# z and products held in PSUM until split, query mixes on VectorE, x words in a ring, new instruction orders

## The chip, the cores and the metric

The program runs on one core of a Trainium2 chip. The metric is the device time of one execution in microseconds (us). Engines are TensorE (PE, matmuls; its weight loads are PEld), VectorE (DVE), ScalarE (ACT), GpSimd (POOL) and SyncE (SP, which here only issues DMAs). Each has its own instruction stream, carried out in order; they meet at semaphores.

## The reference

The input is x of shape (16, 1024, 256) in float32. For each of the 16 batches, with layernorm (LN) over the last axis:

```
x = x + LN(attention(LN(x)))       # q, k, v from W_qkv (768 x 256) and its bias; softmax(q k^T / 16) v
x = x + LN(ffn(LN(x)))             # silu(x Wg^T) * (x Wu^T), then Wd^T; hidden 768, weights int32 / 127
```

## The kernel before, in words

**Two words for a float32.** Matmuls run on float16. Each float32 operand is split into a high word (`h`, a copy to float16) and a low word (`l`, the float32 minus the high word), and a product takes three matmuls: high*high, low*high, high*low (`passes` and `pairs`, line 1026). For nearly every tensor one engine thus writes the high words (ScalarE, the functions named `*_high`), another subtracts to get the low words (GpSimd `*_low`, some on VectorE), and SP issues a DMA transpose of each (`turn_*`).

**Attention.** Q and K are folded into one 256x256 matrix A, so scores are z times x, where z = A x + bias. `project_z` (two banks of PSUM, one per half `dj` of the 256 rows) makes z for half `g` of a batch. From batch 2 on, the scores are made by Winograd's form of Strassen's scheme: seven block products instead of eight, for each pair of 128-row tiles (`pair_first` makes four, `pair_second`, `pair_third` and `pair_last` one each; line 1177). It needs sums of blocks of x (`mix_keys`, words `t`) and of z (`mix_queries`, words `q`). ScalarE copies products from PSUM (`copy_m1`, `copy_u2`, `copy_u3`), VectorE adds others and finds the row maxima (`sum_*`, line 857), ScalarE does `exp`, then `p_high`, `p_low`, `turn_p`. `attend` multiplies the transposed probabilities by x in four units `u` of 12 matmuls per half batch: `u // 2` is the half of the 256 columns (bank 6 or 7, `OB`), `u % 2` the half of the 1024 keys. `o_high` and `o_low` split the result, `project_v` multiplies by the value matrix.

**FFN.** `y_*` functions do the layernorm between. `gate_up` makes one of six hidden chunks `c` of a half batch: gate in PSUM bank `bank`, up in `bank + 1`, eight matmuls of 512 columns. `silu` (ScalarE) writes hf in SBUF, `h_mul` (VectorE, line 963) multiplies it by up, `h_high` and `h_low` split it. `h_low` of chunks 2 and 5 (`HL_ON_VECTOR`) is VectorE's, the others GpSimd's (line 495). `down` (24 matmuls of 256 columns) multiplies by Wd into banks 4 and 5 (`TB`), then `d_stats`, `d_norm`, `d_add`, `add_bias`, `store`.

**z before the change.** `z_high` (ScalarE) writes zTh from PSUM with scale and bias; `z_float` (VectorE, line 842) writes the same in float32 to zw in SBUF; `z_low` (GpSimd, line 405) makes zTl from it; `mix_queries` (GpSimd, lines 445 to 451, four operations of 256 columns) mixes zw in place; `q_high` (ScalarE) and `q_low` (GpSimd, line 422) split it. PSUM banks 0 to 3 hold products or gate_up results, 4 and 5 hold V and down tiles, 6 and 7 hold attention outputs or gate_up results; so one who writes a bank waits for its last reader, which is the wait written in each call.

**Orders.** No planner runs in the kernel: the order of every engine is written out by hand, call by call, for the first batches, a loop `for b in range(1, 13)` and the last three batches. One turn of the loop does the gate stage and FFN of batch b, the scores of batch b + 1 and b + 2 and the attention of b and b + 1. In the loop TensorE's list says what covers what: for pair 3 it was pair_second, pair_third, project_z, pair_last, gate_up with nothing between the first three, each of which waits for a ScalarE copy of the product before.

**x.** `X` is a ring of four half batches in float32 for the residual (`reload`, `x1_add`, `d_add`, `add_bias`, `store`); `xh`, `xl` are the words of x, two whole batches each; `xs` is the normalized x.

Of the kernel before, what the change touches and what calls it, by code (L numbers as in the profile page):

```python
# [44 lines left out]
def sandwich(nc, x_d, wqkv_d, b_d, wg_d, wu_d, wd_d, out_d):  # L45
# [8 lines left out]
    with ctx:  # L54
# [6 lines left out]
        X = two("X", [128, 4, D], f32, 4)  # L61
        xs = sb("xs", [128, NT, D])
        xh, xl = two("xh", [128, NT, D]), two("xl", [128, NT, D])
# [61 lines left out]
        xs_in, x_turned, X_in = sems("xs_in", 2), sems("x_turned", 2), sems("X_in", 4)  # L125
        p_turned, y_turned, stored = sems("p_turned", 3), sem("y_turned"), sems("stored", 4)
# [11 lines left out]
        pv_done, dn_done = sems("pv_done", 4), sems("dn_done", 2)  # L138
# [58 lines left out]
        stage = ((half_words(X[0], 1536), half_words(X[1], 1536)), (half_words(X[2], 1536), half_words(X[3], 1536)),  # L197
# [55 lines left out]
        def pv_wait(e, b, g):  # L253
            e.wait_ge(pv_done[1], 2 * b + g + 1)
            e.wait_ge(pv_done[3], 2 * b + g + 1)

# [12 lines left out]
        def turn_x(s, b, g, low):  # L269
            k, gs = b % 2, slice(4 * g, 4 * g + 4)  # L270
# [6 lines left out]
            s.engine.dma_start_transpose(dst[k][:, gs, :, :].rearrange("p t d n -> p (t d) n"),  # L277
                                         src[k][:, gs, :].rearrange("p t d -> p (t d)")).then_inc(x_turned[g], 16)

        def turn_t(s, b, g, low):  # L280
# [3 lines left out]
            s.wait_ge(bv_ready, 1)  # L284
            scores_read(s, b - 1, 4)
# [3 lines left out]
        def reload(s, b, g):  # L289
            k = (2 * b + g) % 4  # L290
            s.wait_ge(stored[k], 32 * (b // 2))
            if b < 2:
                s.wait_ge(ffn_turned[b], 32)
# [20 lines left out]
        def store(s, b, g, pair):  # L314
            k, pr = (2 * b + g) % 4, slice(2 * pair, 2 * pair + 2)
# [5 lines left out]
        def store_last(s, part):  # L321
            ts = (slice(0, 3), slice(3, 4))[part]
            s.wait_ge(last_out[part], (3, 1)[part])
            s.engine.dma_start(out_d[B - 1, :, :].rearrange("(p t) d -> p t d", t=NT)[:, 4 + ts.start:4 + ts.stop, :], X[3][:, ts, :]
                               ).then_inc(stored[3], 16)
# [52 lines left out]
        def x_hat_first(tile):  # L378

            return X[2 + tile // 4][:, tile % 4, :]  # L380

# [6 lines left out]
        def x_low(p, b, g):  # L388
            k, gs = b % 2, slice(4 * g, 4 * g + 4)
# [5 lines left out]
            pv_wait(p, b - 2, 1)  # L395
            src = xs[:, gs, :] if b else X[2 + g][:, :, :]
            p.engine.tensor_tensor(out=xl[k][:, gs, :], in0=src, in1=xh[k][:, gs, :], op=ALU.subtract
# [19 lines left out]
        def q_low(p, b, g):  # L417
            n = 2 * (b - 2) + g
            p.wait_ge(qh_done, n + 1)
            p.wait_ge(mix_z, 4 * (n + 1))  # L420
# [17 lines left out]

        def mix_queries(e, b, g):

            w = zw[:, :, :].rearrange("p j (u h n) -> p j u h n", h=2, n=128)
            a11, a12, a21, a22 = w[:, 0, :, 1, :], w[:, 1, :, 1, :], w[:, 0, :, 0, :], w[:, 1, :, 0, :]
            n = 4 * (2 * (b - 2) + g)
            zl_wait(e, b, g, 1)
            e.engine.tensor_tensor(out=a22, in0=a22, in1=a21, op=ALU.add).then_inc(mix_z, 1)
            e.wait_ge(mix_z, n + 1)
            e.engine.tensor_tensor(out=a21, in0=a21, in1=a11, op=ALU.subtract).then_inc(mix_z, 1)
            e.wait_ge(mix_z, n + 2)
            e.engine.tensor_tensor(out=a11, in0=a22, in1=a11, op=ALU.subtract).then_inc(mix_z, 1)
            e.wait_ge(mix_z, n + 3)  # L450
            e.engine.tensor_tensor(out=a12, in0=a12, in1=a11, op=ALU.subtract).then_inc(mix_z, 1)
# [109 lines left out]
        def x_high(a, b, g):  # L561
# [5 lines left out]
            pv_wait(a, b - 2, 1)  # L567
            a.engine.activation(xh[b % 2][:, gs, :], xs[:, gs, :] if b else X[2 + g][:, :, :], ACT.Copy).then_inc(xh_done, 1)

        def z_high(a, b, g, bank):  # L570
            a.wait_ge(cb_ready, 1)
            scores_read(a, b - 1, 2 * (g + 1))
            for dj in range(2):
# [33 lines left out]
        def q_high(a, b, g):  # L607
            n = 2 * (b - 2) + g
            a.wait_ge(mix_z, 4 * (n + 1))
# [18 lines left out]
        def o_high(a, b, g, dh):  # L628
            n = 2 * b + g
            a.wait_ge(pv_done[2 * dh + 1], n + 1)  # L630
# [3 lines left out]
        def y_hat(a, b, g, half):  # L634
# [3 lines left out]
            for t in (2 * half, 2 * half + 1):  # L638
                a.engine.activation(yn[:, t, :], X[n % 4][:, t, :], ACT.Identity, bias=nb3[:, t:t + 1], scale=rs3[:, t:t + 1]
# [8 lines left out]
        def silu(a, b, g, c, bank):  # L648
# [3 lines left out]
            if n > 2:  # L652
# [3 lines left out]
        def h_high(a, b, g, c):  # L656
# [4 lines left out]
            a.engine.activation(hTh[g][:, c, :], hf[:, n % 3, :], ACT.Copy).then_inc(hh_done, 1)  # L661

        def add_bias(a, b, g, pair):
            n = 2 * b + g
            k = n % 4
# [6 lines left out]
        def last_bias(a):  # L672
# [5 lines left out]
            for t in range(4):  # L678
                a.engine.activation(X[3][:, t, :], X[3][:, t, :], ACT.Identity, bias=c2[:, n % 4, t:t + 1]).then_inc(last_x, 1)
# [156 lines left out]
        def z_float(v, b, g, bank):  # L836
            v.wait_ge(ql_done, 2 * (b - 2) + g)
            for dj in range(2):
# [4 lines left out]
                                       op0=ALU.mult, op1=ALU.add).then_inc(zw_done, 1)  # L843

# [114 lines left out]
        def h_mul(v, b, g, c, bank):  # L959
# [51 lines left out]
        def last_add(v, *ts):  # L1011
            v.wait_ge(last_rs, 1 + (ts[0] == 3))
            for t in ts:
# [5 lines left out]
                v.engine.scalar_tensor_tensor(out=X[3][:, t, :], in0=last_at(t), scalar=rs4[:, t:t + 1], in1=X[3][:, t, :],  # L1019
# [106 lines left out]

        def first_scores_left(t, banks):
# [86 lines left out]
        def attend(t, b, g, u, free=None, also=None):  # L1214
            dh, q0, k = u // 2, 4 * (u % 2), b % 2
# [9 lines left out]
            passes(t, OB[dh], pairs(*((xh[k][:, kt, ds], xl[k][:, kt, ds], PTh[g][:, kt, :], PTl[g][:, kt, :])  # L1225
                                      for kt in range(q0, q0 + 4))), q0 == 0, q0 == 4).then_inc(pv_done[u], 1)
# [57 lines left out]
        def _(engine):  # L1284
# [1307 lines left out]
```

## Time and profile before

| what | us |
|---|---|
| median of 3 runs (lowest, highest) | 1403.44 (1403.24, 1407.39) |
| the profiled execution, its own time | 1403.3 |
| its span | 1401.4 |
| TensorE busy | 1325.5 (95%) |
| GpSimd busy | 1124.2 (80%) |
| ScalarE busy | 1015.5 (72%) |
| VectorE busy | 956.6 (68%) |

The profiled execution is 0.14 us below the median, so it stands for it. The mean granted TensorE clock is 0.996. A busy time is that of the engine's instructions with overlaps counted once. An idle time in brackets behind an instruction, with a releaser, is time in which the engine stood still before it.

### The profile page before, as it was taken

How to read it: one execution, taken by the hardware profiler on the slowest of the kernel's cores; microseconds unless marked ns; L12 is line 12 of the kernel's file. 1: busy time of each engine (PE TensorE's matmuls, PEld its weight loads, DVE VectorE, ACT ScalarE, POOL GpSimd, SP SyncE). 2: the span in 40 equal slices, each digit the busy share in tenths (PEclk: the TensorE clock that was granted, in tenths of full speed). 3: DMA queues.
4: the chain of work that ended last, by engine and by line, in shares of the span. 5: the costliest groups of instructions: out<-in, count | busy, mean ns of one | idle time of the engine just before them, and what ended most of it. 6: DMA issues, size and time to landing. Idle time of an engine off the chain costs nothing. (4 is left out here: it accounts for less than half of the span.)

```text
span 1401.4 us, 23224 instructions
## 1 busy us (share of the span) xinstructions
PE 1325.5 (95%) x7210; PEld 697.5 (50%) x7210; DVE 956.6 (68%) x2504; ACT 1015.5 (72%) x1602; POOL 1124.2 (80%) x1225
## 2 busy tenths in 40 slices
PE   8988999999999999999999999999999999999997
PEld 4443554454554545455445544545445454555554
DVE  7975576776667666666676766767676677756666
ACT  5657687777777777777777777777777777776746
POOL 5488688797987979979798797978979799795645
PEclk9999999999999999999999999999999999999999
DMA  4876757566566655676556765666666466646612
GB/s 143 195 151 121 128 102 140 115 129 126 120 122 135 129 99 121 128 136 129 112 119 119 130 136 115 127 121 124 136 120 140 103 121 128 128 91 121 143 31 77
DMA packets 492111, 171.97 MB, mean 123 GB/s; under 512 B 473041, under 2 KB 475473, under 8 KB 491986
## 3 DMA queue, kind: packets, MB, share of 16 engines
q1 hardware_dynamic: 491184, 169.67, 60.8%
q8 instruction: 59, 0.97, 0.3%
q10 hardware_dynamic: 802, 0.79, 0.2%
q14 instruction: 66, 0.54, 0.1%
HBM read 36.70 MB, written 16.78 MB: 38 GB/s over the span
## 5 line engine op out<-in xcount | busy, mean ns | idle before, releaser
L459 POOL TENSOR_TENSOR Pl<-P,Ph 128x1024 f16<-128x1024 f32 x96 | 210.1, 2194 | 59.8 <-ACT Ph L626 30.9
L963 DVE SCALAR_TENSOR_TENSOR hf<-S,sc,hf 128x512 f32<-128x512 f32 x192 | 139.8, 745 | 131.8 <-ACT hf L654 117.6
L1026 PE MATMUL S<-PTh,xh 128*128 128x512 f16 x512 | 194.1, 379 | 2.3 <-DMA PTl<-Pl 2.3
L1026 PE MATMUL S<-PTl,xh 128*128 128x512 f16 x512 | 194.1, 379 | 0.0
L1026 PE MATMUL S<-PTh,xl 128*128 128x512 f16 x512 | 194.1, 379 | 0.0
L654 ACT ACTIVATE hf<-S,sc 128x512 f32<-128x512 f32 x192 | 126.9, 682 | 79.5 <-POOL hTl L495 61.6
L495 POOL TENSOR_TENSOR hTl<-hf,hTh 128x512 f16<-128x512 f32 x128 | 166.7, 1317 | 8.5 <-ACT hTh L661 6.1
L1026 PE MATMUL S<-Wh,hTh 128*128 128x256 f16 x768 | 170.3, 273 | 0.8 <-POOL hTl L495 0.7
L1026 PE MATMUL S<-Wh,hTl 128*128 128x256 f16 x768 | 170.3, 273 | 0.0
L1026 PE MATMUL S<-yTh,Gh 128*128 128x512 f16 x384 | 146.8, 382 | 14.5 <-DMA yTl<-yl 6.6
L619 ACT ACTIVATE P<-P,nmx,sc 128x1024 f32<-128x1024 f32 x112 | 138.0, 1233 | 27.3 <-DVE nmx L863 27.1
L360 POOL TENSOR_TENSOR rs<-rs,mhalf 128x4 f32<-128x4 f32 (+2 forms) x160 | 146.0, 912 | 13.3
L626 ACT ACTIVATE Ph<-P 128x1024 f16<-128x1024 f32 x128 | 133.0, 1050 | 32.0 <-DMA PTl<-Pl 31.0
L1026 PE MATMUL S<-yTl,Gh 128*128 128x512 f16 x384 | 146.6, 382 | 0.0
L1026 PE MATMUL S<-yTh,Uh 128*128 128x512 f16 x384 | 146.1, 381 | 0.0
L1026 PE MATMUL S<-yTl,Uh 128*128 128x512 f16 x384 | 146.0, 380 | 0.0
L857 DVE CUSTOM_DVE_ANT_0 P<-S,P 128x512 f32<-128x512 f32 x112 | 76.4, 683 | 80.3 <-ACT P L598 79.0
L661 ACT ACTIVATE hTh<-hf 128x512 f16<-128x512 f32 x192 | 114.8, 620 | 9.8 <-DVE hf L963 9.6
L926 DVE SCALAR_TENSOR_TENSOR S<-S,rinv,bvb 128x256 f32<-128x256 f32 x128 | 53.4, 485 | 99.9 <-PE S L1026 99.9
L356 POOL TENSOR_SCALAR rs<-mv,sc 128x2 f32<-128x2 f32 (+2 forms) x96 | 35.2, 366 | 95.6 <-DVE mv L939 84.4
L857 DVE CUSTOM_DVE_ANT_0 P<-S,P,mxh 128x512 f32<-128x512 f32 x112 | 84.0, 750 | 26.0 <-PE S L1177 17.6
L495 DVE TENSOR_TENSOR hTl<-hf,hTh 128x512 f16<-128x512 f32 x64 | 86.1, 1346 | 13.1 <-ACT hTh L661 13.1
(202 smaller groups left out, 3357.4 us busy)
## 6 DMA issues: line engine op xcount, KB each, us to landing
xs<-in_L_attn_t SPq DMA_DIRECT2D x32, 512.0 KB, 4.6
X<-in_L_attn_t SPq DMA_DIRECT2D x32, 512.0 KB, 4.2
out_x<-X SPq DMA_DIRECT2D x62, 256.0 KB, 3.3
PTh<-Ph SPq DMA_TRANSPOSE x128, 3.5
PTl<-Pl SPq DMA_TRANSPOSE x128, 3.3
hTh<-in_L_ffn_w_up SPq DMA_DIRECT2D x1, 768.0 KB, 8.6
hTl<-in_L_ffn_w_gate SPq DMA_DIRECT2D x1, 768.0 KB, 5.0
hTl<-in_L_ffn_w_down SPq DMA_DIRECT2D x1, 768.0 KB, 6.7
```

Source lines behind the costliest of these rows:

```text
L356: p.engine.tensor_scalar(rs, var, scalar1=eps, scalar2=mul, op0=ALU.add, **({} if mul is None else {"op1": ALU.mult})).then_inc(g_step, 1)
L360: return p.engine.tensor_tensor(out=rs, in0=rs, in1=mhalf[:, 0:rs.shape[1]], op=ALU.pow)
L459: p.engine.tensor_tensor(out=Pl[:, m % 3, :], in0=P[:, m % 4, :], in1=Ph[:, m % 3, :], op=ALU.subtract).then_inc(pl_vector if i in PL_ON_V ...
L495: p.engine.tensor_tensor(out=hTl[g][:, c, :], in0=hf[:, n % 3, :], in1=hTh[g][:, c, :], op=ALU.subtract).then_inc(hl_vector if c in HL_ON_ ...
L619: a.engine.activation(P[:, m % 4, :], ps[:, bank:bank + 2, :].rearrange("p a n -> p (a n)") if b < 2 else P[:, m % 4, :], ACT.Exp, bias=nm ...
L626: a.engine.activation(Ph[:, m % 3, :], P[:, m % 4, :], ACT.Copy).then_inc(ph_done, 1)
L654: a.engine.activation(hf[:, n % 3, :], ps[:, bank, :], ACT.Silu, scale=sc2[:, 3:4]).then_inc(silu_done, 1)
L661: a.engine.activation(hTh[g][:, c, :], hf[:, n % 3, :], ACT.Copy).then_inc(hh_done, 1)
L857: return v.engine.tensor_tensor_reduce(out=out, in0=ps[:, bank, :], in1=other, scale=1.0, scalar=least, op0=ALU.add, op1=ALU.max, accum_ou ...
L926: v.engine.scalar_tensor_tensor(out=y_tile(t), in0=y_tile(t), scalar=rinv[:, b % 2, 4 * g + t:4 * g + t + 1], in1=bvb[:, :], op0=ALU.mult, ...
L963: v.engine.scalar_tensor_tensor(out=hf[:, n % 3, :], in0=ps[:, bank + 1, :], scalar=sc2[:, 4:5], in1=hf[:, n % 3, :], op0=ALU.mult, op1=AL ...
L1026: done = t.engine.matmul(out, s, m, start=(start and i == 0), stop=(stop and i == len(terms) - 1))
```

## The change

1. **z stays in PSUM.** From batch 2 on `z_float` and `z_low` give way to `z_bias` (VectorE, in place in PSUM), `z_high` (ScalarE, now a plain copy that waits for z_bias) and `z_rest` (VectorE). 
2. **`mix_queries` moves from GpSimd to VectorE**, reads z in PSUM and writes zw: five operations of 256 columns in place of four.
3. **Chunks 2 and 5:** `h_mul` writes its product back into the up bank, `h_high` reads it there and `h_rest` (VectorE) takes the place of VectorE's `h_low`.
4. **`attend` is cut in eight `attend_part`s** of 6 matmuls, `project_z` in two `z_part`s (12 each, one bank), so that they can be put between products. The z of half 0 goes to banks 6 and 7 (free when `o_low` is done), that of half 1 to banks 2 and 3.
5. **Rings.** xh and xl become rings of five half batches (2 KB more per partition each), X a ring of three (4 KB less). Setup data that lay in X[3] lies in tTl.
6. **New orders** on all five engines. TensorE executes the same matmuls as before.

```diff
+        def z_bias(v, b, g, bank):
+            for dj in range(2):
+                v.wait_ge(z_done, 4 * b + 2 * g + dj + 1)
+                v.engine.tensor_scalar(ps[:, bank + dj, :], ps[:, bank + dj, :], scalar1=ZS, scalar2=cb[:, dj:dj + 1],
+                                       op0=ALU.mult, op1=ALU.add).then_inc(zw_done, 1)
+
+        def z_rest(v, b, g, bank):
...
+                v.engine.scalar_tensor_tensor(out=zTl[:, dj, g * 512:(g + 1) * 512], in0=ps[:, bank + dj, :], scalar=1.0,
+                                              in1=zTh[:, dj, g * 512:(g + 1) * 512], op0=ALU.mult, op1=ALU.subtract
+                                              ).then_inc(zl_done, 1)
+
+        def mix_queries(v, b, g, bank):
...
+            zl_wait(v, b, g, 1)
+            v.wait_ge(qh_done, n)
+            v.wait_ge(ql_done, n)
...
+            v.engine.tensor_copy(w[:, 0, :, 0, :], at_z(*a21)).then_inc(mix_z, 1)
+            v.wait_ge(mix_z, 5 * n + 1)
+            term(a22, at_z(*a22), w[:, 0, :, 0, :], ALU.add)
+            term(a21, w[:, 0, :, 0, :], at_z(*a11), ALU.subtract)
+            v.wait_ge(mix_z, 5 * n + 2)
+            term(a11, w[:, 1, :, 0, :], at_z(*a11), ALU.subtract)
+            v.wait_ge(mix_z, 5 * n + 4)
+            term(a12, at_z(*a12), w[:, 0, :, 1, :], ALU.subtract)
```

TensorE's loop, from pair 3 to the next batch's first pair, before and after (`free` waits in brackets):

```
before: pair_first 3, project_v 1, pair_second 3, pair_third 3, project_z 0 [u3_copied], pair_last 3,
  gate_up 0,0 | down | gate_up 0,1 0,2 | down | gate_up 0,3 [zw_done] | project_z 1 [silu, hmul 3]
  gate_up 0,4 0,5 1,0 1,1 [zw_done] 1,2 1,3 1,4 1,5 | down | down | pair_first 0
after:  pair_first 3, project_v 1, pair_second 3, z_part 0,0, pair_third 3, z_part 0,1, gate_up 0,0,
  pair_last 3 | down | down | gate_up 0,1 0,2 0,3 0,4 [mix_z 4 and 5] | z_part 1,0 [silu 4], z_part 1,1 [hmul 4]
  gate_up 0,5 [silu 3, hl_vector 1] 1,0 1,1 [hl_vector 2] 1,2 | down | gate_up 1,3 [mix_z 9 and 10]
  gate_up 1,4 1,5 [silu, hmul 10] | down | pair_first 0 [silu 11, hmul 11, silu 12, hl_vector 4],
  attend_part 4, pair_second 0, attend_part 0, pair_third 0, attend_part 6 5 1 7, pair_last 0
```

In SP's list `turn_y` of batch 0 moves from behind two reloads and two setup transposes to directly behind the transposes of x of batch 2, and `reload` of half 1 of batch 1 moves far back. In ScalarE's loop three `h_high` of half 1 and `q_high` of half 1 move ahead of the next batch's products; GpSimd's `y_low` moves ahead of `x_low`, and `q_low` of half 1 ahead of the second pair's products.

## Rows read from the trace of the kernel before

**Rows 1.** Page, busy time of each engine over the span:
```profile
PE 1325.5 (95%) x7210; PEld 697.5 (50%) x7210; DVE 956.6 (68%) x2504; ACT 1015.5 (72%) x1602; POOL 1124.2 (80%) x1225
```

**Rows 2.** Windows: stretch, length, then busy us of each engine, granted clock, DMA:
```profile
595.90:681.60 85.70, 81.65 (x445) 42.76 (x446) 58.44 (x156) 64.22 (x103) 72.40 (x78) 1.00 0.64 124
618.00:655.00 37.00, 36.20 (x214) 20.55 (x212) 26.86 (x54) 28.50 (x45) 35.07 (x37) 1.00 0.68 133
...
107.00:124.00 17.00, 12.53 (x46) 5.10 (x47) 4.01 (x8) 10.13 (x17) 11.27 (x11) 0.80 0.74 126
```

**Rows 3.** Timeline of TensorE (start, duration, instruction): unbroken runs, first and last:
```profile
565.17 0.27 PE L1026 MATMUL S<-Wh,hTh 128*128 128x256 f16 x1
...
570.19 0.27 PE L1026 MATMUL S<-Wh,hTh 128*128 128x256 f16 x1
...
577.05 0.38 PE L1026 MATMUL S<-PTh,xh 128*128 128x512 f16 x1
...
582.01 0.38 PE L1026 MATMUL S<-PTh,xl 128*128 128x512 f16 x1
```

**Rows 4.** Timeline of TensorE: its stops in one turn of the loop:
```profile
595.86 0.38 PE L1177 MATMUL S<-tTh,qTh 128*128 128x512 f16 x1 [1.16 <-issue]
...
615.61 0.39 PE L1177 MATMUL S<-tTh,qTh 128*128 128x512 f16 x1 [0.69 <-ACT P L592]
...
617.21 0.38 PE L1026 MATMUL S<-xTh,Ah 128*128 128x512 f16 x1 [0.78 <-ACT P L598]
...
621.41 0.39 PE L1026 MATMUL S<-yTh,Gh 128*128 128x512 f16 x1 [0.80 <-DMA yTl<-yl]
...
670.89 0.39 PE L1177 MATMUL S<-tTh,qTh 128*128 128x512 f16 x1 [0.50 <-ACT P L586]
...
681.59 0.38 PE L1177 MATMUL S<-tTh,qTh 128*128 128x512 f16 x1 [1.16 <-issue]
```

**Rows 5.** Timeline of GpSimd: the q_low ahead of the first stop of rows 4:
```profile
593.63 2.13 POOL L422 TENSOR_TENSOR qTl<-zw,qTh 128x1024 f16<-128x1024 f32 x1
```

**Rows 6.** Groups of VectorE (busy us, mean ns of one):
```profile
L963 DVE SCALAR_TENSOR_TENSOR hf<-S,sc,hf 128x512 f32<-128x512 f32 x192 | 139.8, 745 | 131.8 <-ACT hf L654 117.6 <-PE S L1026 13.8
L495 DVE TENSOR_TENSOR hTl<-hf,hTh 128x512 f16<-128x512 f32 x64 | 86.1, 1346 | 13.1 <-ACT hTh L661 13.1
...
L926 DVE SCALAR_TENSOR_TENSOR S<-S,rinv,bvb 128x256 f32<-128x256 f32 x128 | 53.4, 485 | 99.9 <-PE S L1026 99.9
...
L842 DVE TENSOR_SCALAR zw<-S,cb 128x512 f32<-128x512 f32 x64 | 45.1, 745 | 20.7 <-POOL qTl L422 13.7 <-ACT zTh L575 5.3 <-issue 1.6
...
L914 DVE SCALAR_TENSOR_TENSOR oTl<-S,oTh 128x512 f16<-128x512 f32 x64 | 42.6, 682 | 0.9 <-ACT oTh L632 0.7
...
L1019 DVE SCALAR_TENSOR_TENSOR X<-zw,rs,X 128x256 f32<-128x256 f32 x4 | 1.8, 480 | 0.2
```

**Rows 7.** Groups of GpSimd:
```profile
L405 POOL TENSOR_TENSOR zTl<-zw,zTh 128x512 f16<-128x512 f32 x60 | 68.1, 1155 | 1.3 <-DVE zw L842 1.2
...
L445 POOL TENSOR_TENSOR zw<-zw 128x256 f32<-128x256 f32 x28 | 20.8, 744 | 1.1
```

**Rows 8.** Groups of ScalarE:
```profile
L654 ACT ACTIVATE hf<-S,sc 128x512 f32<-128x512 f32 x192 | 126.9, 682 | 79.5 <-POOL hTl L495 61.6 <-PE S L1026 14.1 <-DVE hTl L495 3.4
L661 ACT ACTIVATE hTh<-hf 128x512 f16<-128x512 f32 x192 | 114.8, 620 | 9.8 <-DVE hf L963 9.6
...
L611 ACT ACTIVATE qTh<-zw 128x1024 f16<-128x1024 f32 x28 | 29.4, 1049 | 0.0
```

**Rows 9.** Timeline of TensorE in the first batches:
```profile
107.36 0.38 PE L1026 MATMUL S<-xTh,Ah 128*128 128x512 f16 x1 [2.83 <-ACT P L619]
...
114.22 0.61 PE L1026 MATMUL S<-yTh,Gh 128*128 128x512 f16 x1 [4.11 <-DMA yTl<-yl]
```

**Rows 10.** Timeline of GpSimd, the y_low of batch 0's first half:
```profile
101.66 2.13 POOL L486 TENSOR_TENSOR yl<-yn,yh 128x1024 f16<-128x1024 f32 x1
```

**Rows 11.** Timeline of SP, where SPq is the issue of a DMA:
```profile
106.83 1.84 SPq L311 DMA_TRANSPOSE yTl<-yl  x1
```

More of the change, by code:

```diff
@@ new lines, in _ @@
+            y_high(a, 1, 0)
+            x_high(a, 3, 1)
+            copy_u2(a, 2, 3)
+            copy_u3(a, 2, 3)
+            exp(a, 2, 4)
+            exp(a, 2, 5)
+            exp(a, 2, 6)
+            p_high(a, 2, 4)
+            silu(a, 1, 0, 0, 0)
+            z_high(a, 3, 0, 6)
+            h_high(a, 1, 0, 0)
+            silu(a, 1, 0, 1, 2)
+            y_hat(a, 1, 1, 0)
+            y_hat(a, 1, 1, 1)
+            h_high(a, 1, 0, 1)
+            y_high(a, 1, 1)
+            silu(a, 1, 0, 2, 0)
@@ new lines, in _ @@
+                copy_u3(a, b + 2, 3)
+                p_high(a, b + 2, 4)
+                exp(a, b + 2, 5)
+                exp(a, b + 2, 6)
+                silu(a, b + 1, 0, 0, 0)
+                p_high(a, b + 2, 5)
+                z_high(a, b + 3, 0, 6)
+                t_high(a, b + 3, 0)
+                h_high(a, b + 1, 0, 0)
+                silu(a, b + 1, 0, 1, 2)
+                y_hat(a, b + 1, 1, 0)
+                y_hat(a, b + 1, 1, 1)
+                y_high(a, b + 1, 1)
+                silu(a, b + 1, 0, 2, 0)
@@ L1975, in _ @@
             y_high(a, 15, 1)
-            h_high(a, 15, 0, 0)
-            silu(a, 15, 0, 1, 0)
             silu(a, 15, 0, 2, 2)
@@ new lines, in _ @@
+            sum_12(v, 2, 1)
+            o_low(v, 1, 0, 0)
+            p_low(v, 2, 1)
+            y_scale(v, 1, 0, 0)
+            y_scale(v, 1, 0, 1)
+            y_stats(v, 1, 0, 0)
+            y_stats(v, 1, 0, 1)
+            sum_11(v, 2, 2)
+            row_inverse(v, 1, 1)
+            x1_add(v, 1, 0, 0)
+            x1_add(v, 1, 0, 1)
+            sum_21(v, 2, 2)
+            sum_22(v, 2, 2)
+            sum_12(v, 2, 2)
+            o_low(v, 1, 1, 0)
+            o_low(v, 1, 1, 1)
+            sum_11(v, 2, 3)
@@ new lines, in _ @@
+            y_scale(v, 1, 1, 0)
+            y_scale(v, 1, 1, 1)
+            y_stats(v, 1, 1, 0)
+            y_stats(v, 1, 1, 1)
+            sum_21(v, 2, 3)
+            sum_22(v, 2, 3)
+            x1_add(v, 1, 1, 0)
+            x1_add(v, 1, 1, 1)
+            z_bias(v, 3, 0, 6)
+            sum_12(v, 2, 3)
+            h_mul(v, 1, 0, 0, 0)
+            d_stats(v, 0, 1, 0)
+            z_rest(v, 3, 0, 6)
+            h_mul(v, 1, 0, 1, 2)
+            mix_queries(v, 3, 0, 6)
+            h_mul(v, 1, 0, 2, 0)
@@ L2223, in _ @@
-            h_mul(v, 13, 1, 3, 2)
-            h_mul(v, 13, 1, 4, 6)
-            h_low(v, 13, 1, 2)
-            d_add(v, 12, 1, 1)
-            h_mul(v, 13, 1, 5, 0)
-            d_stats(v, 13, 0, 0)
+                d_add(v, b, 0, 0)
+                sum_21(v, b + 2, 1)
+                sum_22(v, b + 2, 1)
+                sum_11(v, b + 2, 1)
+                sum_12(v, b + 2, 1)
+                row_inverse(v, b + 1, 0)
+                o_low(v, b + 1, 0, 0)
+                p_low(v, b + 2, 1)
@@ new lines, in _ @@
+                row_inverse(v, b + 1, 1)
+                y_scale(v, b + 1, 0, 0)
+                y_scale(v, b + 1, 0, 1)
+                y_stats(v, b + 1, 0, 0)
+                y_stats(v, b + 1, 0, 1)
+                sum_11(v, b + 2, 2)
+                x1_add(v, b + 1, 0, 0)
+                x1_add(v, b + 1, 0, 1)
+                sum_21(v, b + 2, 2)
+                sum_22(v, b + 2, 2)
+                o_low(v, b + 1, 1, 1)
+                sum_12(v, b + 2, 2)
+                o_low(v, b + 1, 1, 0)
@@ new lines, in _ @@
+                sum_11(v, b + 2, 3)
+                y_scale(v, b + 1, 1, 0)
+                y_scale(v, b + 1, 1, 1)
+                y_stats(v, b + 1, 1, 0)
+                y_stats(v, b + 1, 1, 1)
+                sum_21(v, b + 2, 3)
+                sum_22(v, b + 2, 3)
+                x1_add(v, b + 1, 1, 0)
+                x1_add(v, b + 1, 1, 1)
+                z_bias(v, b + 3, 0, 6)
+                sum_12(v, b + 2, 3)
+                h_mul(v, b + 1, 0, 0, 0)
+                z_rest(v, b + 3, 0, 6)
```

1477 lines of the change are left out of this document (732 added, 745 removed).

## The prediction

> **What bounds the kernel now.** I read the page's busy times first [rows 1]: TensorE is busy for 1325.5 of 1401.4 us, GpSimd, the next, for 80%. So TensorE bounds it, and since the change leaves its matmuls as they are, only its lost time can be won. The timeline gives the pace at which it issues without a stop [rows 3]: 23 steps of 512 columns in 582.01 - 577.05 = 4.96 us, 0.2157 us each, and 46 steps of 256 columns in 5.02 us, 0.1091 each. One turn of the loop has 300 matmuls of 512 columns (attend 96, gate_up 96, products 84, z 24) and 144 of 256 (down 96, V 48): 300 x 0.2157 + 144 x 0.1091 = 80.4 us. The turn lasts from the stop at 595.86 to the same stop at 681.59 [rows 4], 85.7 us. It loses 5.3 us, and there are (1300 - 189) / 85.7 = 13 such turns: 69 us. The windows view of one turn [rows 2] says where the others are full: in the gate stage (618 to 655) GpSimd works 35.1 of 37.0 us, ScalarE 28.5, VectorE 26.9. In the first batches TensorE stops for 2.83 and 4.11 us [rows 9], and in the window around it the granted clock is 0.80 of full: after those stops it stood at its level of 1.2 GHz for a while, in place of 2.4 [rows 2].
>
> **The stops that go.** Each stop costs its idle time and 0.16 us of drain (512 columns take 0.38 us, the pace is 0.2157).
> - 1.16 us before the second pair's products [rows 4]: they need the low q words, and GpSimd's q_low runs from 593.63 to 595.76 [rows 5]; TensorE goes on at 595.86. In the new order q_low stands before the work of the pair, and GpSimd is relieved by 4 z_low (1.155) and 8 mixes (about 0.73) a turn [rows 7], 10.5 us of 72.4 [rows 2]. Gone: 1.3 us.
> - 0.69 and 0.78 us before pair_third and z [rows 4]: nothing lay between a product and ScalarE's copy of it. Now a z_part, 6 x 0.2157 = 1.3 us, lies between, and 1.3 is more than 0.69 + 0.16. Gone: 1.8 us.
> - 0.80 us for yTl [rows 4]: y_low was queued behind two x_low; now it is ahead of x_low. Gone: 0.9 us. The same for 0.50 us before pair_second [rows 4], if the copy of the first product is on time. With the smaller stops at gate_up that makes 5.3.
>
> **What the change adds.** VectorE: 4 z_rest, which resemble o_low (PSUM and float16 in, float16 out, 0.682), and 10 operations of 256 columns from PSUM, nearest to y_scale at 0.485 (512 columns at 0.745 are the upper bound, as the pieces are strided; nothing the lower) [rows 6]: 2.7 + 4.9 us. z_bias costs as much as z_float (0.745). h_rest takes 0.682 in place of 1.346 [rows 6]: 2.7 us less. VectorE goes from 58.4 to 63.3 us a turn, within 80.4. But the gate stage decides: there it goes from 26.9 to 26.9 + 7.6 - 2.0 (three h_low) + 0.7 (a fourth) = 33 us, against a stage of 12 gate_ups (1.73 each), 4 downs (2.6), 2 z_parts and a product: 34.4 us. ScalarE: 28.5 + 3 h_high (0.62) + q_high (1.05) [rows 8] = 31.4 us of 34.4. Both have 1.5 to 3 us of slack, so the order within the stage counts.
>
> The Trainium skill (VectorE: DVE Perf Modes, "The TRN2 errata") gives an operation from PSUM 62 cycles more than one from SBUF, and its rules say to copy PSUM to SBUF first where many operations follow. The rows do not bear it out: 256 columns from PSUM take 485 ns and from SBUF 480 [rows 6]; by the page the 18 operations would cost about 1.2 us more a turn.
>
> **Walk through the gate stage,** with T = 0 at gate_up 0,0, durations of the rows above, every queue in its new order.
> - VectorE ends y_stats at about -0.4, sum_21 and sum_22 of pair 3 at 1.3 (pair_last at 1.7 does not wait), two x1_add at 4.7, z_bias 6.1, sum_12 7.1 (gate_up 0,1 at 7.6 waits for it), z_high on ScalarE 7.7, z_rest 9.2.
> - silu 1 ends at 10.0, h_mul 1 at 10.8, the five mixes at 13.2; gate_up 0,4 wants their banks at 12.8 and its second at 13.7: about 0.
> - ScalarE then does y_hat and y_high (3.1) before silu 2, so silu 3 ends at 15.15; z_part 1,0 wants its bank at 14.5: **0.7 lost**.
> - h_high 5 ends at 21.3 and h_rest 5 at 22.4; gate_up 1,1 wants that bank at 22.1: **0.4**.
> - The second mix ends at 28.5, its banks are wanted from 27.7: **0.4**.
> - h_rest 5 of half 1 ends at 37.3 and is wanted at 37.2; then ScalarE loads its exp table, does exp 7 and copy_m1 to 39.9, and pair_second waits: **0.4** together.
> - In the attention stage one attend_part (1.3) or two stand between a product and the next, against 0.9 to 1.6 us of copy, queue and sum; p_low 7 ends some 1.3 us before its words are wanted. I allow **0.6**, and 0.4 for handovers in the stage that the walk takes as free.
>
> Together 2.9 us a turn, so 5.3 - 2.9 = 2.4 saved, times 13 = 31 us. The rings cost nothing while their covers hold: reload of X waits for a store of three half batches back, with some 12 us to x1_add and 8 us needed; if that cover is gone a turn pays up to the 4.2 us of a reload.
>
> **The first batches.** y_low ends at 103.8 [rows 10], but SP issued its transpose only at 106.8 [rows 11] behind reloads, and the words came at 114.2 [rows 9]. In the loop yl's end to gate_up takes 4.6 us, so the words can be there at 108.4. The z ahead of it no longer waits for exp (2.83), so it is done by 107. gate_up starts 5.8 us earlier, and with under 2 us of idle left I expect no drop of the clock: 0.20 of 17 us [rows 2] is 3.4 us. Together 9 us. The last batches lose only about 1 us; I take them as the same.
>
> **Sum:** 1403.3 (span 1401.4 and 1.9 around it) - 31 - 9 = **1363 us**, 2.9% less. The profiled execution is within 0.2 us of the median 1403.44.
>
> **Rivals.**
> - *Half the gain.* ScalarE, with 31.4 of 34.4 us full, is late at each silu: every stop of the walk grows, to 4.2 us a turn in place of 2.9. 13 x 1.1 = 14, and 6 of the first batches: 1383. For it: every bank waits for a silu within one gate_up of it. Against: half of its old waits for GpSimd (61.6 us over the span, at silu) go [rows 8].
> - *Slower.* The mix is the one long piece between z and the banks of gate_up 0,4 and 1,3. If its operations take 0.745 (the upper bound) and each handover 0.15, a turn has 10 x 0.41 = 4.1 us more in VectorE's gate stage, 37 of 34.4: VectorE bounds the stage, all of it is on the path, and a turn loses 7.0. 13 x 1.7 - 9 = +13: 1416. It decides from about 6.0 us lost a turn, 3.1 above my walk. For it: the stage has no more than 1.5 us of slack. Against: 485 ns in the row of the nearest shape.
> - *Nothing.* The stops only move, as each order was already made to hide what it could: 5 us a turn lost again, y held up by another item of SP: 1403.
> - *More.* The stops of the walk fall within 0.3 us of zero each and some vanish: 1.2 a turn, 13 x 4.1 + 9: 1341.
>
> **Chances.** My forecast (1350 to 1376) 0.46, half the gain (1376 to 1398) 0.25, more 0.12, slower 0.11, nothing 0.06. The range reaches from 1342 to 1398, over the first three cases but for the far side of *more*; it leaves out that (0.04) and the two last (0.17). A measurement can tell 0.3%, 4.2 us, from no change: faster 0.82, same 0.07, slower 0.11.
>
> **What would show it.** Right: TensorE still busy about 1320 us; turns of 82 to 84 us; no stop at the copies of pair 3, at yTl or at the second pair's fourth product; VectorE at 33 of about 36 us in the gate stage, GpSimd under 30; mixes of 0.45 to 0.5 us; granted clock 1.00 after the first z_parts. Wrong: stops before gate_up for zw (the mixes) of over 1 us in each turn; mixes of 0.7; x1_add waiting for X; or a turn under 81.5 or over 85.

## The result and the profile after

The changed kernel takes **1357.16 us** (median, 1356.33 to 1359.70) against 1404.24 us for the kernel before: a ratio of 0.9664, 95% interval 0.9643 to 0.9685, 3.4% less. The forecast was 1363.0 with a range of 1342 to 1398. The execution that was profiled took 1356.33 us, its span is 1354.4.

Busy times of the whole span, from the page of the changed kernel, beside [rows 1]:
```profile
PE 1319.2 (97%) x7210; PEld 703.3 (52%) x7210; DVE 998.7 (74%) x2700; ACT 1009.2 (75%) x1602; POOL 941.6 (70%) x1057
```
TensorE does the same 7210 matmuls. GpSimd, the fullest of the others before (1124.2 us), is now the least full of them: 182.6 us of its work went, and VectorE took over only 42.1.

The windows view: one turn of the loop, its gate stage, the first gate_ups, and the last 50 us. Columns: stretch, length, busy us of PE, PEld, DVE, ACT and POOL, granted clock, DMA share, GB/s. The first three answer to [rows 2]:
```profile
665.57:747.40 81.83, 81.80 (x450) 43.66 (x451) 61.74 (x172) 64.94 (x105) 60.16 (x69) 1.00 0.62 132
675.53:711.00 35.47, 35.47 (x212) 20.74 (x213) 31.85 (x79) 31.92 (x51) 30.61 (x34) 1.00 0.59 123
107.00:124.00 17.00, 17.00 (x79) 7.26 (x78) 11.63 (x19) 15.67 (x26) 14.23 (x11) 1.00 0.76 153
1300.00:1352.00 52.00, 41.75 (x264) 26.28 (x264) 31.80 (x82) 28.03 (x52) 27.08 (x40) 0.92 0.19 49
```
In the gate stage TensorE is busy for all of 35.47 us. The other three have 3.5 to 4.9 us left there, where GpSimd had 1.9 before. In the first batches the clock stays at 1.00, its level of 2.4 GHz, where it was 0.80 on average. In the last row it is 0.92: that stretch got worse.

The timeline of TensorE shows which stops are left: three of the kind that the loop still has, the one at the first gate_up, and two in the last batch, beside [rows 4, 9]:
```profile
583.47 0.39 PE L1233 MATMUL S<-xTh,qTh 128*128 128x512 f16 x1 [1.19 <-DVE mxs L896]
...
665.57 0.39 PE L1233 MATMUL S<-xTh,qTh 128*128 128x512 f16 x1 [0.98 <-DVE mxs L896]
...
1154.64 0.39 PE L1233 MATMUL S<-xTh,qTh 128*128 128x512 f16 x1 [1.26 <-DVE mxs L896]
...
106.50 0.39 PE L1074 MATMUL S<-yTh,Gh 128*128 128x512 f16 x1 [0.32 <-DMA yTl<-yl]
...
1300.61 0.27 PE L1074 MATMUL S<-Vh,oTh 128*128 128x256 f16 x1 [1.62 <-DVE oTl L953]
...
1307.99 0.61 PE L1074 MATMUL S<-yTh,Gh 128*128 128x512 f16 x1 [4.60 <-DMA yTl<-yl]
```
From 583.47 to 1154.64 are seven turns: 81.6 us each, 1.2 above the 80.4 of TensorE's pace. In these turns all stops of [rows 4] are gone. What took their place is one stop, at the last product of the third pair (pair_last), which waits for VectorE's sums.

Held against that pace (0.2157 and 0.1091 us a matmul, the rest of the distance from one start to the next counted as lost), TensorE lost 18.1 us from 30 to 150 us before and loses 8.6 now; from there to 1300 us 64, now 19; in the last batch 1.2, now 9.0, with the stop around 1300 us. The first 30 us are the same. So the head gave 9.5, the middle 45, and the tail took back 8. The spans differ by 47.0.

Why pair_last is late stands in VectorE's timeline and in SP's queue, one turn:
```profile
658.23 0.08 DVE L896 DVE_READ_ACCUMULATOR2_ANT mxh<- 128x1 f32 x1
660.60 0.88 DVE L987 SCALAR_TENSOR_TENSOR X<-S,rs,X 128x256 f32<-128x256 f32 x2 [2.29 <-DMA X<-in_L_attn_t]
...
664.76 0.75 DVE L896 CUSTOM_DVE_ANT_0 P<-S,P,mxh 128x512 f32<-128x512 f32 x1
```
```profile
641.06 0.58 SPq L321 DMA_DIRECT2D out_x<-X  x1
650.88 2.62 SPq L309 DMA_TRANSPOSE PTh<-Ph  x2
653.54 1.33 SPq L278 DMA_TRANSPOSE xTh<-xh  x1
654.91 0.58 SPq L298 DMA_DIRECT2D X<-in_L_attn_t  x1
```
The first x1_add (L987) waits 2.29 us for a reload of X. The two sums that pair_last needs stand behind it and end at 665.5; pair_last goes on at 665.57. The reload was issued at 654.91, although SP had been idle from 641.6 to 650.9: it stands in the queue behind two transposes that wait for P.

### The profile page after: what moved, and what is told of

It reads as the page before. It is cut to its first block and busy times, and to the rows that moved or that the text cites. A ratio compares the mean times of both kernels' runs of the same rounds, so it can differ in the third digit from the quotient of the medians.

```text
span 1354.4 us, 23106 instructions
## 1 busy us (share of the span) xinstructions
PE 1319.2 (97%) x7210; PEld 703.3 (52%) x7210; DVE 998.7 (74%) x2700; ACT 1009.2 (75%) x1602; POOL 941.6 (70%) x1057
## 5 line engine op out<-in xcount | busy, mean ns | idle before, releaser
L449 POOL TENSOR_TENSOR Pl<-P,Ph 128x1024 f16<-128x1024 f32 x96 | 205.4, 2146 | 83.0 <-issue 45.8
L485 POOL TENSOR_TENSOR hTl<-hf,hTh 128x512 f16<-128x512 f32 x128 | 149.0, 1169 | 47.5 <-ACT hTh L658 44.4
L1002 DVE SCALAR_TENSOR_TENSOR hf<-S,sc,hf 128x512 f32<-128x512 f32 x128 | 95.4, 746 | 32.0 <-ACT hf L651 16.5
L360 POOL TENSOR_SCALAR rs<-mv,sc 128x2 f32<-128x2 f32 (+2 forms) x96 | 30.7, 320 | 117.3 <-DVE mv L978 102.9
L476 POOL TENSOR_TENSOR yl<-yn,yh 128x1024 f16<-128x1024 f32 x32 | 68.2, 2133 | 32.6 <-ACT yh L641 32.6
L1074 PEld LDWEIGHTS S<-Wh,hTh 128*128 128x128 f16 x768 | 75.1, 98 | 15.0 <-issue 2.8
```

What stands on the lines that cost most here:

```text
L360: p.engine.tensor_scalar(rs, var, scalar1=eps, scalar2=mul, op0=ALU.add, **({} if mul is None else {"op1": ALU.mult})).then_inc(g_step, 1)
L449: p.engine.tensor_tensor(out=Pl[:, m % 3, :], in0=P[:, m % 4, :], in1=Ph[:, m % 3, :], op=ALU.subtract).then_inc(pl_vector if i in PL_ON_V ...
L476: p.engine.tensor_tensor(out=yl[:, :, :], in0=yn[:, :, :], in1=yh[:, :, :], op=ALU.subtract).then_inc(yl_done, 1)
L485: p.engine.tensor_tensor(out=hTl[g][:, c, :], in0=hf[:, n % 3, :], in1=hTh[g][:, c, :], op=ALU.subtract).then_inc(hl_vector if c in HL_ON_ ...
L1002: v.engine.scalar_tensor_tensor(out=ps[:, bank + 1, :] if c in HL_ON_VECTOR else hf[:, n % 3, :], in0=ps[:, bank + 1, :], scalar=sc2[:, 4: ...
L1074: done = t.engine.matmul(out, s, m, start=(start and i == 0), stop=(stop and i == len(terms) - 1))
```

## The experiments

Every run is compared with the kernel before, on the same chip; differences to the changed kernel are to its 1357.16 us.

**1. The reload, alone.**
```
                 store(s, b - 1, 1, 1)
+                reload(s, b + 1, 0)
                 turn_p(s, b + 2, 2, 0)
                 turn_p(s, b + 2, 1, 0)
                 turn_x(s, b + 3, 0, 0)
-                reload(s, b + 1, 0)
```


> The changed kernel with one item of SP's queue moved: the reload of X for half 0 stands right behind the last store of the batch before (where SP idles from 641.6 to 650.9 us in the profile of the changed kernel) and no longer behind two transposes of P and one of x. My theory: the stops that are left before the last product of the third pair (9.1 us in 12 stops, PE <- DVE mxs) come from x1_add, which waits up to 2.3 us for that reload and stands ahead of the sums on VectorE. Then all 12 go with 0.16 us of drain each: 11 us less than the changed kernel, 1346, and VectorE's wait for X falls from 21.5 us to under 5. Rival A: VectorE is simply behind at that place; then x1_add starts earlier but the stops shrink by less than half: 1352 to 1357. Rival B: the reload now makes SP wait for the store to land and holds up the transposes of P behind it: a new stop before the attention products, 1357 or more.

Measured: **1339.86 us**, ratio 0.9548 (0.9533 to 0.9563), 17.3 less than the changed kernel. Waits of TensorE for that sum fall from 9.1 us in 12 stops to 0.2 in one, and VectorE waits no more for X. The windows view of 2.6 turns has no idle time of TensorE at all:
```profile
850.00:1060.00 210.00, 210.00 (x1152) 112.16 (x1151) 158.73 (x443) 164.50 (x264) 151.09 (x171) 1.00 0.63 133
```
The theory holds and its sum was low by 6. The 12 stops with their drain are 11.0. Another 1.7 is a stretch behind the longest of them (2.07 us, at 502.27), where the granted clock of the changed kernel was 0.78 over 7.7 us:
```profile
502.30:510.00 7.70, 7.63 (x39) 4.59 (x40) 3.81 (x11) 5.28 (x8) 4.57 (x3) 0.78 0.51 105
```
Some 3 us more were handovers of 0.14 to 0.28 us at the next V and gate_up, most of which go too. The last 1.6 us of the 17.3 are not placed.

**2. The last batches, alone.** TensorE's order; the other queues follow it, GpSimd does P's last low words before a norm, and y_low of half 0 is VectorE's:
```
-            gate_up(t, 14, 1, 2, ...)
             down(t, 14, 0, 0, ...)
             down(t, 14, 0, 1, ...)
             attend_part(t, 15, 0, 1)
             attend_part(t, 15, 0, 2)
-            gate_up(t, 14, 1, 3, ...)
-            gate_up(t, 14, 1, 4, ...)
             attend_part(t, 15, 0, 3)
-            gate_up(t, 14, 1, 5, ...)
+            gate_up(t, 14, 1, 2, ...)
             project_v(t, 15, 0, ...)
...
             attend_part(t, 15, 1, 7)
+            gate_up(t, 14, 1, 3, ...)
             project_v(t, 15, 1, ...)
+            gate_up(t, 14, 1, 4, ...)
+            gate_up(t, 14, 1, 5, ...)
```


> The changed kernel with only the last two batches reordered: three gate_ups of batch 14 (chunks 3, 4, 5 of half 1) stand behind the first V projection of batch 15 again, two of them behind the second, with their silus and products in the other queues, and y_low of the last batch's half 0 is on VectorE. My theory: the 8.9 us that TensorE loses after 1300 us (1.1 in the kernel before) come from the missing cover: with V ending 5.2 us earlier and 5.2 us of work moved behind it, the stop of 4.6 us for the low words of y falls under 2, that of 1.6 for o goes, and the half clock after them goes: 5 to 7 us less than the changed kernel, 1350 to 1352. Rival: the stop is the latency of y's own chain or of its transposes, whatever stands beside it: 1355 to 1358. A third way: the words of the last P row come too late for attention products that now start earlier, a new stop of 1 to 4 us: 1354 to 1357.

Measured: **1350.05 us**, ratio 0.9613 (0.9598 to 0.9627), 7.1 less. TensorE's stops in the last batch are now:
```profile
1301.49 0.39 PE L1074 MATMUL S<-yTh,Gh 128*128 128x512 f16 x1 [0.32 <-DMA yTl<-yl]
...
1305.91 0.27 PE L1074 MATMUL S<-Wh,hTh 128*128 128x256 f16 x1 [0.79 <-DVE X L987]
...
1318.86 0.39 PE L1074 MATMUL S<-yTh,Gh 128*128 128x512 f16 x1 [0.64 <-DMA yTl<-yl]
```
The 4.60 and 1.62 are gone. So is what the clock cost there: in the changed kernel it was granted at 0.68 over the 7.6 us behind the stop of 4.60 (2.4 us), here it is 1.00. The chain from V to the words of y is as long as ever (19.5 us in the changed kernel, 1288.5 to 1308.0; 19.9 here, 1281.6 to 1301.5); what had been lost was the work beside it.

**3. Both.**


> Both edits together, the early reload and the reordered last batches. They lie in different stretches of the time, so they should add up: 16 to 18 us less than the changed kernel, 1339 to 1341. If either is a story, what it does alone shows again here.

Measured: **1334.81 us**, ratio 0.9507 (0.9492 to 0.9523), the fastest kernel of this study: 22.4 less than the changed kernel, where the two alone gave 17.3 + 7.1 = 24.4. They lie in different stretches and nearly add up. TensorE is busy for 98% of the span.

**4. One cover of the change undone.**
```
                 pair_second(t, b + 1, 3)
-                z_part(t, b + 2, 0, 0, 6, ...)
                 pair_third(t, b + 1, 3)
+                z_part(t, b + 2, 0, 0, 6, ...)
                 z_part(t, b + 2, 0, 1, 7, ...)
```


> The changed kernel with the first half of z (6 matmuls, 1.3 us) put back behind the third product of the last pair, as before the change, so that nothing lies between the second product and the third. My theory: the stop of 0.69 us and its 0.16 of drain come back in each of 13 turns, 11 us more than the changed kernel: 1368. Rival: with ScalarE's queue otherwise ordered the copy would be in time without the cover: within 2 us of 1357. A second: the shift by 1.3 us also makes later things late (the bank of gate_up 0,0 waits for a copy), 15 us more or over: 1372.

Measured: **1366.12 us**, ratio 0.9733 (0.9718 to 0.9749), 9.0 more. The table of TensorE's waits (us in total, times, longest) has the old stop back:
```profile
PE S L1233 <- ACT P L587: 11.9, 13, 1.0
```
The edit reaches the loop's 12 turns; the 13th of these stops, of 0.69 us behind the loop, the changed kernel has too. The copy is no earlier than before the change; only the matmuls in between hide it.

**5 and 6. A dearer mix.** The first copy of each mix is repeated in place, two or five times:
```
+            for _ in range(5):
+                v.engine.tensor_copy(w[:, 0, :, 0, :], at_z(*a21)).then_inc(v_step, 1)
+                v.wait_ge(v_step, v.tick(v_step))
             v.engine.tensor_copy(w[:, 0, :, 0, :], at_z(*a21)).then_inc(mix_z, 1)
```


> The changed kernel with the first copy of each query mix made three times over, in place (2 more operations of 256 columns, 0.41 us each and a handover, 0.9 us a mix, 1.8 us a turn on VectorE). VectorE works 31.9 of the 35.5 us of its gate stage in the profile of the changed kernel. If the load of the stage is what counts (my rival 'slower'), 33.7 still fits in 35.5 and nothing changes: within 1.5 us of 1357. If the place counts, the first mix ends at 687.7 and gate_up 0,4 wants its banks at about 688.3, the second at 702.1 against 703.2: the first is 0.3 late, 0.16 of drain beside it, the second on time: 0.5 a turn, 6 us more: 1363.

> The same with 5 more copies a mix, which doubles its price: 2.25 us each, 4.5 us a turn, close to the 4.1 us by which my rival 'slower' had the mix dearer. By load, VectorE's gate stage goes to 36.4 of 35.5 us: 0.9 late a turn and some 0.3 of drain, 13 x 1.2 = 16 us more, 1373. By place, the first mix is 1.65 late and the second 1.15, with 0.16 of drain each: 3.1 a turn, 40 us more, 1397. By the rival's own sum (all of it on the path) 13 x 4.1 = 53 more, 1410.

Measured: **1361.33 us** (ratio 0.9691, 0.9674 to 0.9709) with two, 4.2 more; **1398.03 us** (0.9954, 0.9942 to 0.9966) with five, 40.9 more. The interval with two overlaps that of the changed kernel (0.9643 to 0.9685), so what shows its price is the trace: 14 new stops for the mixes, of 0.31 us mostly, 4.3 us in all. They stand at the second bank, though, not at the first, as I had expected. With five TensorE stops at both banks that the mixes hold. The two together are as long as expected, 2.8 us, but the lengths are changed round, 1.13 at the first (1.65 expected) and 1.69 at the second (1.15 expected):
```profile
709.50 0.39 PE L1077 MATMUL S<-yTh,Gh 128*128 128x512 f16 x1 [1.13 <-DVE zw L864]
...
725.20 0.39 PE L1077 MATMUL S<-yTh,Gh 128*128 128x512 f16 x1 [1.69 <-DVE zw L864]
```
So the place decides, not the load: the sum by load said +16, that by place +40. Had the mixes been as dear as the rival *slower* took them, 4.1 us a turn more, they would have cost about this much.

**7. The products of chunks 2 and 5 in SBUF again**, with h_low on VectorE in place of h_rest; in half 1 and in the second batch the low words of chunk 2 stand before the product of chunk 5. The up bank is free here as soon as the product is made.
```
-  out=ps[:, bank + 1, :] if c in HL_ON_VECTOR else hf[:, n % 3, :]
+  out=hf[:, n % 3, :]
...
-                h_mul(v, b, 1, 5, 2)
                 h_rest(v, b, 1, 2, 6)
+                h_mul(v, b, 1, 5, 2)
```


> The changed kernel with the products of chunks 2 and 5 in SBUF again and VectorE's h_low (1.346 us) in place of h_rest (0.682), the bank free once the product is read; in half 1 the low words of chunk 2 stand ahead of the product of chunk 5, since the ring of three products would lock otherwise. VectorE has 4 x 0.66 = 2.7 us a turn more, of which 1.3 in half 1 behind the mixes, and silu waits for low words again. If that kept product in PSUM is worth what the load says (34.5 of 35.5 us still fits): within 2 us of 1357. If place and silu's waits count, each h_low delays what stands behind it (a sum, z_bias, the next product) by 0.66: I expect 0.3 to 0.8 us a turn, 4 to 10 us more: 1361 to 1367.

Measured: **1361.88 us**, ratio 0.9695 (0.9682 to 0.9708), 4.7 more, at the low end. The interval touches that of the changed kernel (0.9643 to 0.9685); the trace has one new stop of TensorE, at the first pair's second product (0.33 us, 13 times, 4.4 us in all), which agrees with it. The price that I had put on h_low was wrong, though. One row of that kernel and one of the kernel before, each "min/median/max" in ns:
```profile
L1009 DVE TENSOR_TENSOR hTl<-hf,hTh x64: 671/704/1944, 117.9 to 1350.5; 128x512 f16<-128x512 f32 x64
```
```profile
L495 DVE TENSOR_TENSOR hTl<-hf,hTh x64: 672/1488/2247, 129.1 to 1390.2; 128x512 f16<-128x512 f32 x64
```
The same operation takes 0.67 us at best in both; its mean of 1.346 [rows 6] came from half of them taking twice that and more. With GpSimd relieved its mean is 0.844, so h_rest saves 4 x 0.16 us a turn of VectorE's time here, not 4 x 0.66.

**8. GpSimd's q_low first, in the kernel before.**
```
-                x_norm(p, b + 3, 1)
                 q_low(p, b + 2, 1)
+                x_norm(p, b + 3, 1)
```


> The kernel before, with two items of GpSimd's queue swapped: q_low for half 1 ahead of the norms of x (2.4 us of small operations) that stood in front of it. My step said that the stop of 1.16 us before the second pair's products is GpSimd's q_low ending at 595.76, and cost 1.3 us with its drain. Then 13 x 1.3 = 17 us less than before: 1387. Rival: GpSimd is so full (35.1 of 37.0 us of the gate stage) that what is moved back makes another stop, at the norms or p_low: under 8 us less, 1396 or more.

Measured: **1404.28 us**, ratio 0.9999 (0.9991 to 1.0008): nothing. q_low ended 2.5 us earlier and TensorE stopped at the same place, for another releaser. VectorE's, GpSimd's and TensorE's timelines of this kernel:
```profile
591.49 2.85 DVE L459 TENSOR_TENSOR Pl<-P,Ph 128x1024 f16<-128x1024 f32 x1
594.26 0.74 DVE L857 CUSTOM_DVE_ANT_0 P<-S,P,mxh 128x512 f32<-128x512 f32 x1
```
```profile
591.13 2.13 POOL L422 TENSOR_TENSOR qTl<-zw,qTh 128x1024 f16<-128x1024 f32 x1 [0.56 <-ACT qTh L611]
```
```profile
595.16 0.38 PE L1177 MATMUL S<-tTh,qTh 128*128 128x512 f16 x1 [1.01 <-DVE mxs L857]
```
and VectorE's in the kernel before, where GpSimd did small norms at that time:
```profile
592.04 1.21 DVE L459 TENSOR_TENSOR Pl<-P,Ph 128x1024 f16<-128x1024 f32 x1
```
The low words of P (p_low) on VectorE take 2.85 us when q_low runs beside them and 1.21 when it does not. In the kernel before the sum behind them was done at 593.9, 0.8 us before TensorE wanted its bank (595.86 - 1.16 = 594.7); now it is done at 595.0, 0.9 after it is wanted (595.16 - 1.01 = 594.15). q_low was the right wait, and moving it alone made another of nearly the same length, 1.01 us for 1.16.

**9. q_low first, and the sum ahead of p_low.**
```
-                p_low(v, b + 1, 1)
                 sum_12(v, b + 1, 1)
+                p_low(v, b + 1, 1)
```


> The kernel before with q_low ahead of the norms (which alone gave nothing: VectorE's low words of P then ran beside q_low and took 2.85 us in place of 1.21, and the sum behind them was late) and, new, that sum (of the first pairs' third product) ahead of those low words on VectorE. Then neither q_low (ends 593.3) nor the sum (about 594.0) is late for the product at 594.0, and the stop of 1.2 us goes. But ScalarE's copy of the next pair's first product waits for the same low words of P, which now end at about 595.3: the second product would be 0.6 late, with 0.16 of drain. I expect 0.4 a turn left of the gain, 5 us less than before: 1399. If that copy is not late: 13 x 1.2 = 15 less, 1389. If the low words again run beside another GpSimd operation and take 2.8 us: a stop of 2 us at the copy, 8 us or more above before: 1412.

Measured: **1395.66 us**, ratio 0.9933 (0.9920 to 0.9946), 9.3 less than before. The stop at that product is gone, and ScalarE's copy of the next pair's first product is late as expected, by 0.33 us where I expected 0.6:
```profile
596.03 0.39 PE L1177 MATMUL S<-tTh,qTh 128*128 128x512 f16 x1 [0.33 <-ACT P L586]
```
So the stop of 1.16 us was worth its time only to a change that also moves p_low. The changed kernel does: there p_low stands behind both sums and an o_low.

**10. The words of the first y first, in the kernel before.**
```
+            turn_y(s, 0, 0, 0)
+            turn_y(s, 0, 0, 1)
             reload(s, 1, 0)
-            turn_y(s, 0, 0, 0)
             reload(s, 1, 1)
-            turn_y(s, 0, 0, 1)
```


> The kernel before, with two reloads of X behind the two transposes of the first y on SP's queue, not between them. My step said that the stop of 4.11 us at the first gate_up is SP's order (yl ends at 103.8, its transpose is issued at 106.8), not y's chain. The stop of 2.83 before z stays; V and z end at about 110.1, the words can be there at 107: so 4.1 us less, and if the half clock after it is the child of both stops, part of the 3.4 it costs goes as well: 4 to 7.5 us less than before, 1397 to 1400. Rival: the words come no earlier, since the transpose itself waits for other transfers: within 1.5 us of 1404.

Measured: **1398.52 us**, ratio 0.9955 (0.9942 to 0.9969), 6.4 less. The stop of 4.11 us is gone, that of 2.83 stays, and the window around them reads 1.00 in the clock, where [rows 2] has 0.80:
```profile
107.00:124.00 17.00, 16.03 (x75) 6.83 (x74) 8.41 (x11) 14.91 (x23) 16.59 (x13) 1.00 0.79 146
```

**11. The mixes on GpSimd again**, in the changed kernel (four operations there, as before the change), with one copy of both banks by VectorE:
```
-            v.engine.tensor_copy(w[:, 0, :, 0, :], at_z(*a21)).then_inc(mix_z, 1)
...
+            v.engine.tensor_copy(zw[:, :, :], ps[:, bank:bank + 2, :]).then_inc(mix_z, 1)
```


> The changed kernel with the query mixes on GpSimd again: VectorE copies both banks of z to zw in one operation (about 1.2 us in place of 2.05), GpSimd mixes there with four operations (0.73 us each, 2.9 a mix) as before the change; z's split stays in PSUM; q_high of half 1 stands some places later on ScalarE. GpSimd's gate stage goes from 30.6 to 36.4 of 35.5 us, VectorE's from 31.9 to 30.3. If the relief of GpSimd is the larger part of the gain, its low words of h come late, silu waits for them and TensorE for silu: 2 to 5 us a turn, 26 to 65 more than the changed kernel: 1383 to 1422. Rival: the order alone made the gain, and GpSimd's idle time takes the mixes up: 1357 to 1363.

Measured: **1479.18 us**, ratio 1.0523 (1.0507 to 1.0540), 122 more, almost twice what I had as the most. ScalarE's waits say where it went:
```profile
ACT qTh L620 <- POOL zw L441: 122.2, 26, 6.3
```
GpSimd does the mix behind y_low, an h_low and a norm, and q_high holds ScalarE for up to 6.3 us with the silus queued behind it; TensorE then stops up to 4.6 us for a silu. I had summed the load (36.4 of 35.5 us) and not walked the handover. Nor had I counted the clock: behind four of the stops of 4.4 us (at 292.96, 383.13, 474.78 and 567.78) it was granted at 0.58 to 0.76 over the next 7 us, and its mean over the run is 0.971, where the changed kernel has 0.995. By these means, as an estimate, some 35 of the 122 us are the clock's. This run doesn't tell load from order: with orders made for it the mix on GpSimd would cost less, how much less is open. The ring of five for x's words was not taken back by itself, since the new orders lean on it, nor a fourth tile given to X.

## Why the prediction was right, point by point

- **"Only its lost time can be won", pace 80.4 a turn**: right. With the reload early, TensorE runs a stretch of 210 us without an idle moment.
- **The stops that go**: all went. *Copies of pair 3*: shown by experiment 4, 9.0 us for one of the two, where 13 x 0.85 = 11 was the sum (10 for the 12 turns that the edit reaches). The other one, before z, was not tried. *yTl, pair_second*: gone in the trace, not tried singly. *q_low*: the wait was named rightly, but experiment 8 shows that moving q_low alone is worth nothing, since p_low beside it then makes the sum late. The change escapes that only because it moves p_low as well, which my step did not look at.
- **5.3 lost a turn before**: somewhat high. From 255.18 to 1108.07 the same stop comes every 85.3 us, so 4.9 a turn; the turn that I read was one of the longer ones.
- **What the change adds, 2.9 a turn**: too much, it is 1.2, and the place was wrong. This is the largest miss of the sum: 4.9 - 1.2 = 3.7 saved a turn, where 2.4 stood. The walk had 1.9 us of it in the gate stage, and there is none. Its steps were late by about 1 us: the first mix ends 12.2 us after gate_up 0,0 (forecast 13.2, wanted at 12.8), silu 3 at 14.1 (forecast 15.15, wanted at 14.5). One cause is the price of the mix: 10 operations at 0.485 stand in the sum, and they take 0.41 to 0.42:
```profile
L864 DVE SCALAR_TENSOR_TENSOR zw<-S,zw 128x256 f32<-128x256 f32 x56 | 23.7, 424 | 1.9
L864 DVE SCALAR_TENSOR_TENSOR zw<-zw,S 128x256 f32<-128x256 f32 x56 | 20.7, 411 | 0.0
```
- **h_rest, 2.7 us a turn less on VectorE**: mis-sized. It is 0.64 us (experiment 7); the 1.346 of h_low was no price but a mean with waits in it.
- **Loads of the gate stage**: VectorE 33 of 34.4 forecast, 31.85 of 35.47 measured; ScalarE 31.4, 31.92; GpSimd under 30, 30.61. Good to 1.2 us.
- **"The rings cost nothing while their covers hold"**: this is the step that failed. The cover did not hold: SP issues the reload behind two waiting transposes, x1_add waits for X in 13 places, and it costs 17.3 us in all, the largest loss that the runs found in the changed kernel. I had named the sign (x1_add waiting for X) and priced a turn's worst case at 4.2 us, but worked the cover out from durations, without walking SP's new queue.
- **VectorE on PSUM**: the rule of the Trainium skill (VectorE: DVE Perf Modes, "The TRN2 errata") was not borne out here either: 256 columns from PSUM take 411 to 424 ns in the mix. The nearest pair of the same form, with a scalar read from a tile, is x1_add in the changed kernel, with a PSUM operand (a median of 473 ns, 128 times), and the 480 ns from SBUF of [rows 6].
- **First batches, 9 us**: right in the sum, 9.5 us, not in its parts. Gate_up starts at 106.50, not at 114.22, so 7.7 us earlier where 5.8 was forecast, and the clock stays up. Of the 3.4 us that the clock was said to cost, 0.8 fell on the idle time: it was granted at 0.80 from 110.2 to 114.2, where TensorE did nothing, and at 0.55 from 114.3 to 120.0. Experiment 10 bears out SP's order as the cause of the 4.11, and gives 6.4 us of the 9.
- **"The last batches [...] the same"**: wrong by 7.8 us. The new order puts three gate_ups ahead of the V projections of batch 15 that had stood behind the first of them and covered y's chain; experiment 2 gives 7.1 of it back.
- **Rivals**: *slower* rightly took the mix for the dangerous piece: experiment 6 lays about its price on the mixes and loses nearly the whole gain. Its condition, operations of 0.745 us, did not hold (0.41 to 0.42). *More* is what the gate stage did, while the reload and the tail took 24 us back. 1363 was nearly right because the terms missed on both sides: -14 in the middle, +8 in the tail. That they partly cancelled is luck.
- **What stays open**: no run takes z's place in PSUM, the relief of GpSimd and the new orders apart. Experiments 4, 9 and 10 show what an order is worth by itself, 6 to 9 us each; experiment 11, meant for the relief, mixes it with an order that was made for the other engine.

## What to carry to other kernels

- A wait that a profile blames is the last of several. Before counting its time as won, ask when the others end and what the moved work will run beside: here the next one had 0.8 us to spare, and the move took that and more (experiments 8 and 9).
- Slack is a matter of place. The stage had 3.6 us of free VectorE, and 0.9 us more at the mix already stopped TensorE. Walk the deadline of each bank, and walk the DMA queue with it: the item that waits for nothing stands behind those that do.
- When work is moved ahead, look at what it used to cover where it stood, above all in the last turn, where nothing follows to take its place.

## What the hardware showed that was not expected

- **VectorE can wait for GpSimd when both have only SBUF operands.** p_low takes 1.21 us alone and 2.85 beside q_low (experiment 8): q_low ends at 593.26, p_low at 594.34, as if it had begun only then. h_low has a mean of 1.346 us beside a full GpSimd and 0.844 beside a relieved one (experiment 7). The forms with a PSUM operand keep their time: 64 h_rests take 677 to 693 ns. The last row is the changed kernel's:
```profile
L1011 DVE SCALAR_TENSOR_TENSOR hTl<-S,hTh x64: 677/680/693, 116.3 to 1343.3; 128x512 f16<-128x512 f32 x64
```
The Trainium skill (SBUF — State Buffer, "SBUF: two separate sides") says that a VectorE operation with two SBUF inputs and a GpSimd operation that reads SBUF take turns on a shared pair of ports, each for a whole instruction. By that rule p_low would end 1.21 us after q_low, at 594.47; the trace agrees within 0.13. A small operation did not hold p_low up, though: in the kernel before, GpSimd's L360 (128 x 4) ran from 591.50 to 592.52, and p_low, begun at 592.04, took its 1.21. The next small one of GpSimd, at 592.60, took 0.72 us there and 0.20 in experiment 8, where no p_low ran beside it. So a value kept in PSUM is also out of GpSimd's way, a side of this change that neither the diff nor my sum had.
- **The clock after a stop.** Two stops, of 2.83 and 4.11 us, were followed by a stretch at a mean of 0.80; with the second taken away, and one of 2.84 us left at 105.20, it read 1.00 (experiment 10). In the changed kernel the stop of 2.07 at 502.27 was followed by 0.78 over 7.7 us, the stop of 4.60 at 1307.99 by 0.68 over 7.6 us, but one of 2.29 at 51.35 by 1.00, and so were those of the loop at 415.80, 583.47, 665.57, 827.92, 990.88 and 1154.64, up to 1.26 us. So a stop can cost more than its length, and its length alone does not say whether it will.
